# Routed layers: results scattered to their tokens' slots as they are made, and read back by plain loads

## What is computed

```python
x = x + jnp.tanh(g_xattn[i]) * _Li_xattn_ref(_layernorm(x), ctx, ...)
x = x + jnp.tanh(g_ffn[i])   * _Li_ffn_ref(_layernorm(x), ...)
```

```python
scores = jax.nn.softmax((xt @ gate_w.T).astype(jnp.float32), axis=-1)
_, idx = jax.lax.top_k(scores + gate_bias, TOPK)
weights = jnp.take_along_axis(scores, idx, axis=1)
y = jnp.zeros_like(xt)
for e in range(N_EXPERTS):
    gate_e = jnp.sum(jnp.where(idx == e, weights, 0.0), axis=1)
    h = jax.nn.silu(xt @ w1[e].T) * (xt @ w3[e].T)
    y = y + gate_e[:, None] * (h @ w2[e].T)
z = jax.nn.silu(xt @ sw1.T) * (xt @ sw3.T) @ sw2.T
return (y + z).reshape(shape)
```

## Time and profile before

| | before |
|---|---|
| median of three runs | 1986.92 us |
| lowest, highest | 1980.81, 1989.0 us |
| span of the profiled execution | 2007.2 us |
| busy: TensorE, VectorE, ScalarE, GpSimd | 1773.6, 1262.0, 975.4, 528.7 us |
| moved by SyncE's queue, by GpSimd's | 146.00, 30.69 MB |

### The profile page before, as it was taken

How to read it: one execution, slowest core, us unless ns; L and a number is a source line. 1 busy time by engine, 2 the same in 40 slices (tenths; PEclk the granted TensorE clock), 3 DMA queues, 4 the chain that set the end, 5 groups by cost and what they waited for, 6 DMA issues and landing times. The chain is left out here.

```text
span 2007.2 us, 32563 instructions
## 1 busy us (share of the span) xinstructions
PE 1773.6 (88%) x11808; PEld 1447.6 (72%) x11808; DVE 1262.0 (63%) x2310; ACT 975.4 (49%) x1739; POOL 528.7 (26%) x492
## 2 busy tenths in 40 slices
PE   6998899967799996699999969998899789798895
PEld 4667799922577775699999558886577566688884
DVE  6886488546245553588887566765434688656643
ACT  4652476413687671377776234443433255317730
POOL 2220343254333341222220630002000144213333
PEclk9998799988799996699999979999699899899997
DMA  3003377420100000567775220000000100026742
GB/s 109 17 17 126 121 255 248 132 61 0 49 1 12 6 12 25 203 225 229 246 238 169 81 102 1 1 1 1 22 1 1 57 12 12 30 79 208 235 127 81
DMA packets 97139, 178.32 MB, mean 89 GB/s; under 512 B 25184, under 2 KB 61946, under 8 KB 95914
## 3 DMA queue, kind: packets, MB, share of 16 engines
q1 hardware_dynamic: 85496, 146.00, 22.0%
q0 software_dynamic: 11232, 30.69, 5.2%
q10 hardware_dynamic: 288, 0.00, 0.0%
HBM read 149.38 MB, written 27.26 MB: 88 GB/s over the span
## 5 line engine op out<-in xcount | busy, mean ns | idle before, releaser
L1667 POOL DMA_INDIRECT f_block_rows_home<-normed_x,f_token_of_sb x138 | 168.3, 1220 | 451.4 <-PE psum L1713 324.5
L1693 PE MATMUL psum<-f_block_h_sb,f_w1h_home 128*128 128x256 f32 x736 | 211.4, 287 | 30.2 <-issue 10.7
L1693 PE MATMUL psum<-f_block_l_sb,f_w1h_home 128*128 128x256 f32 x736 | 206.8, 281 | 0.0
L1693 PE MATMUL psum<-f_block_h_sb,f_w1l_home 128*128 128x256 f32 x736 | 206.7, 281 | 0.0
L2316 PE MATMUL psum<-a_xT_home,context_w 128*128 128x256 f32 x704 | 182.2, 405 | 13.6 <-PEq L122 9.7
L1703 PE MATMUL psum<-f_w2h_home,f_hidden_h_home 128*128 128x256 f32 x644 | 187.4, 291 | 2.0 <-DVE f_hidden_l_home L1887 1.0
L1703 PE MATMUL psum<-f_w2h_home,f_hidden_l_home 128*128 128x256 f32 x644 | 181.7, 282 | 0.0
L1703 PE MATMUL psum<-f_w2l_home,f_hidden_h_home 128*128 128x256 f32 x644 | 181.7, 282 | 0.0
L1693 PEld LDWEIGHTS psum<-f_block_h_sb,f_w1h_home 128*128 128x128 f32 x736 | 140.8, 191 | 38.5 <-issue 28.6
L2316 PEld LDWEIGHTS psum<-a_xT_home,context_w 128*128 128x128 f32 x704 | 132.6, 198 | 45.3 <-issue 20.0
L2481 ACT ACTIVATE a_probsT_sb<-psum 77x1024 f32<-77x1024 f32 (+1 forms) x128 | 130.7, 1021 | 69.0 <-PE psum L2368 66.5
(11 more groups left out here) (314 smaller groups left out, 3986.6 us busy)
## 6 DMA issues: line engine op xcount, KB each, us to landing
f_w_sb<-in_f_w SPq DMA_DIRECT2D x161, 512.0 KB
sorted_y<-f_result_sb SPq DMA_DIRECT2D x69, 256.0 KB
normed_x<-f_xn_all SPq DMA_DIRECT2D x24, 256.0 KB, 2.1
f_b_row_sb<-in_f_b SPq DMA_DIRECT2D x46, 128.0 KB
f_w_sb<-in_f_w SPq DMA_DIRECT2D x23, 256.0 KB
f_block_rows_home<-normed_x,f_token_of_sb POOLq DMA_INDIRECT x138
residual<-in_x SPq DMA_DIRECT2D x8, 256.0 KB, 6.2
context_w<-in_a_wk SPq DMA_DIRECT2D x2, 1024.0 KB, 5.0
```

The lines of the kernel that those rows point to most:

```text
L1667: nc.gpsimd.indirect_dma_start(block_rows[b % 2][:, h, :], None, xs, bass.IndirectOffsetOnAxis(ap=column, axis=0)).then_inc(sems[f"rows_in ...
L1693: last = nc.tensor.matmul(hid_ps(q)[:, m, :], w, rhs, start=(j == 0), stop=(j == len(parts) - 1))
```

## The change

- A second table `slot_of` gives each row of each block a slot: that of its token's first or second choice, or a place of its own for a pad (from a table `pads` made once). It costs one operation of VectorE ahead of `token_of` and two behind it; the table `rows` and its cast go.
- `sorted_y` becomes `slots`, 4096 slots in the tokens' order with room for pads behind them. SyncE no longer stores results. GpSimd scatters each block, two scatters of 128 rows, when `result_out` says that it is made; it first issues the gathers of four blocks, then for each block b the gathers of block b+4 and the scatters of block b.
- `take_result` waits for both scatters of the block before last instead of the one store; six initial stores that raised its semaphore go, and four bodies of the loop are written out ahead of it in place of DEPTH.
- After the last scatter SyncE reads the slots back by plain loads of 256 KB, one for two tiles and one choice, 16 in a layer. In f0 there is room for 8 at first, and `slots_left` issues the other 8 as combinations free it. `combine` waits for these.
- In f0 and f1, SyncE waits for result b before it loads w2 of the last unit of block b+DEPTH. (Before, the same wait stood ahead of the store, behind both weights.)
- GpSimd's powers in f1 come one after another, with no gathers between them, and the null key and value of the next attention are loaded ahead of `slots_left`.

```diff
@@ find_rows
-        nc.vector.tensor_copy(t["rows"][:], rows_f[:].rearrange("p k t -> p (k t)")).then_inc(sems["rows_done"], 1)
...
+        step.did(nc.vector.tensor_scalar(unfilled[:], source[:], 0.0, None, ALU.is_equal))
         step.then(nc.vector.tensor_scalar(source[:], source[:], -1.0, 0.0, ALU.add, ALU.max))
         step.then(nc.vector.tensor_scalar(wrapped[:], source[:], float(TOKENS), -float(TOKENS), ALU.is_ge, ALU.mult))
         nc.vector.tensor_tensor(t["token_of"][:], source[:], wrapped[:], ALU.add).then_inc(sems["table_done"], 1)
+        step.then(nc.vector.tensor_tensor(unfilled[:], unfilled[:], env["pads"][:], ALU.mult))
+        nc.vector.tensor_tensor(t["slot_of"][:], source[:], unfilled[:], ALU.add).then_inc(sems["slots_done"], 1)
@@ routed_experts
+    LEAD = 4
...
-    RING = 8 if own else 16
...
+    RING = min(len(pairs), 2 * NBATCH)
@@ take_result
-        engine.wait_ge(sems[f"stored{s % 2}"], uses(i, s) * 16 + STORED0)
+        if not (isinstance(b, int) and b < 2):
+            engine.wait_ge(sems[f"stored{s % 2}"], uses(i, s) * (16 * BT))
@@ sync, weights
                 sp.dma_start(w1[k][:], dram[f"{name}_w1"][unit]).then_inc(sems[f"w_in{k}"], 16)
+                if freed and not silu and u == per_expert - 1:
+                    sp.wait_ge(sems["result_out"], (b - DEPTH) + (R0 + 1 + RESULT0))
                 sp.dma_start(w2[k][:], dram[f"{name}_w2"][unit]).then_inc(sems[f"w_in{k}"], 16)
@@ sync, body
-            sp.wait_ge(sems["result_out"], b + (R0 + 1 + RESULT0))
-            sp.dma_start(ys[bass.ds(b * BLOCK, BLOCK), :].rearrange("(h p) d -> p h d", p=P),
-                         result[s % 2][:]).then_inc(sems[f"stored{s % 2}"], 16)
             if what:
                 biases(what, s)
 
         run(sp, body)
+        for s in range(2):
+            sp.wait_ge(sems[f"stored{s}"], 16 * BT * len(range(s, BLOCKS, 2)))
+        for j in range(RING):
+            load_slots(sp, j)
+
+    def load_slots(sp, j):
+
+        b, k = divmod(j, 2)
+        first = k * TOKENS + b * SEQ
+        sp.dma_start(pairs[j % RING], slots[first:first + SEQ, :].rearrange("(h p) d -> p h d", p=P)).then_inc(
+            sems[f"slot_in{j % RING}"], 16)
+
+    def slots_left(sp):
+
+        for j in range(RING, 2 * NBATCH):
+            b, k = divmod(j - RING, 2)
+            sp.wait_ge(sems["combined"], (b * TPB + TPB - 1) * 2 + k + 1)
+            load_slots(sp, j)
@@ gpsimd
-        for s in range(2):
-            pool.wait_ge(sems[f"stored{s}"], STORED0 + 16 * len(range(s, BLOCKS, 2)))
+        def scatter(b):
+            pool.wait_ge(sems["result_out"], b + (R0 + 1 + RESULT0))
+            for h in range(BT):
+                column = t["slot_of"][:, b * BT + h:b * BT + h + 1]
+                nc.gpsimd.indirect_dma_start(slots, bass.IndirectOffsetOnAxis(ap=column, axis=0),
+                                             result[b % 2][:, h, :], None).then_inc(sems[f"stored{b % 2}"], 16)
+
+        for b in range(4):
+            gather(b)
+        pool.wait_ge(t["slots_done"], 1)
+        for b in range(BLOCKS):
+            if b + 4 < BLOCKS:
+                gather(b + 4)
+            scatter(b)
         rows = t["ahead"]["rows"] if t["ahead"] and t["ahead"]["between"] else None
-        for j in range(2 * TILES):
-            if j >= RING:
-                pool.wait_ge(sems["combined"], j - RING + 1)
-            if rows and j >= 8 and j % 4 == 0:
-                rows["power"](pool, j // 4 - 2, batch_tiles(j // 4 - 2))
-            col = (j % 2) * TILES + j // 2
-            nc.gpsimd.indirect_dma_start(gathered[j % RING], None, ys,
-                                         bass.IndirectOffsetOnAxis(ap=t["rows"][:, col:col + 1], axis=0)).then_inc(
-                                             sems[f"gathered{j % RING}"], 16)
-        for b in range(NBATCH - 2 if rows else NBATCH, NBATCH):
+        for b in range(NBATCH if rows else 0):
             rows["power"](pool, b, batch_tiles(b))
@@ combine
-            dve.wait_ge(sems[f"gathered{j % RING}"], 16 * (j // RING + 1))
+            pair = tile // TPB * 2 + k
+            dve.wait_ge(sems[f"slot_in{pair % RING}"], 16 * (pair // RING + 1))
```

More of the change, by code:

```diff
@@ L143, in build @@
         counting, marks = resident("counting", [P, P + 1]), resident("marks", [P, MARKS])
-        codes = resident("codes", [P, 2 * TILES])
+        codes, pads = resident("codes", [P, 2 * TILES]), resident("pads", [P, 2 * BLOCKS])
         context_w = resident("context_w", [P, 4 * DC * D * 2])
@@ L443, in load, with load_null @@
             sp.dma_start(dst, src).then_inc(sems["loaded"], 16)
+    def load_null(sp):
+        for dst, src in null:
+            sp.dma_start(dst, src).then_inc(sems["null_in"], 16)
     def load_late(sp):
         rows["load_late"](sp)
-        for dst, src in null:
-            sp.dma_start(dst, src).then_inc(sems["null_in"], 16)
         if hd == 64:
@@ L758, in vector @@
                 values_out(dve, j)
-    return dict(own=own, load_early=load_early, load=load, load_late=load_late, normalise_start=normalise_start,
+    return dict(own=own, load_early=load_early, load=load, load_null=load_null, load_late=load_late, normalise_start=normalise_start,
                 normalise_power=normalise_power, normalise_apply=normalise_apply, turn=turn, turned_out=turned_out,
@@ L973, in _ @@
                 t["operands_left"](sp)
+                ahead["load_null"](sp)
+                t["slots_left"](sp)
                 ahead["load_late"](sp)
             else:
+                t["slots_left"](sp)
                 t["store_output"](sp)
@@ L1474, in routed_experts @@
     nc, dram, psum, x, ident = env["nc"], env["dram"], env["psum"], env["x"], env["ident"]
-    xs, ys = env["normed_x"], env["sorted_y"]
+    xs, slots = env["normed_x"], env["slots"]
     name, per_expert = cfg["name"], cfg["per_expert"]
@@ L1517, in routed_experts @@
     result = [sb(f"result{s}", [P, BT, D]) for s in range(2)]
-    gathered = [w1[j // 4][:].rearrange("p c i -> p (c i)")[:, j % 4 * D:(j % 4 + 1) * D] for j in range(RING)]
+    whole = result + block_T + [v[:, k:k + BT, :] for v in w2[0:0 if own else len(w2)] for k in range(0, HC, BT)]
+    pairs = [v[:].rearrange("p a d -> p (a d)").rearrange("p (h d) -> p h d", d=D) for v in whole]
+    pairs += [v[:, c, :].rearrange("p (h d) -> p h d", d=D) for v in w1[0:2 if own else len(w1)] for c in range(DC)]
+    RING = min(len(pairs), 2 * NBATCH)
     def rows_places(attention):
@@ L1541, in routed_experts @@
          "block_low", "rounded", "lowered", "rows_in1", "stored0", "stored1"]
-        + [f"{kind}_in{k}" for k in range(DEPTH * per_expert) for kind in "wb"] + [f"gathered{k}" for k in range(RING)])}
+        + [f"{kind}_in{k}" for k in range(DEPTH * per_expert) for kind in "wb"] + [f"slot_in{k}" for k in range(RING)])}
     OUT = 1 if silu else HB
-    MULTIPLIED0, HIDDEN0, RESULT0, STORED0, READY0 = 2, 2 * OUT, 1, 16, 2 * HB
+    MULTIPLIED0, HIDDEN0, RESULT0, READY0 = 2, 2 * OUT, 1, 2 * HB
     hid_ready = sems["hid_ready"]
@@ L1556, in run @@
         rounds = (BLOCKS - max(DEPTH, 3)) // DEPTH
-        for b in range(DEPTH):
-            body(b, 0, b, max(DEPTH, 3))
-        with engine.Fori(1, rounds) as i:
+        for b in range(LEAD):
+            body(b, b // DEPTH, b % DEPTH, max(DEPTH, 3))
+        with engine.Fori(LEAD // DEPTH, rounds) as i:
             for s in range(DEPTH):
@@ L1661, in gpsimd, with gather @@
         pool.wait_ge(t["table_done"], 1)
-        for b in range(BLOCKS):
+        def gather(b):
             if b >= 2:
@@ L1930, in combine @@
                 nc.vector.bn_stats(env["stats"][:, tile - 1, :], x[:, tile - 1, :]).then_inc(sems["stated"], 1)
-            nc.vector.scalar_tensor_tensor(x[:, tile, :], gathered[j % RING],
+            nc.vector.scalar_tensor_tensor(x[:, tile, :], pairs[pair % RING][:, tile % TPB, :],
                                            t["chosen_gates"][:, k, tile:tile + 1], x[:, tile, :],
@@ L2130, in _ @@
             step.then(nc.vector.tensor_scalar(position[:], counting[:, P:P + 1], 1.0, None, ALU.add))
+            step.then(nc.vector.tensor_scalar(env["pads"][:], marks[:, 0:2 * BLOCKS], float(2 * TOKENS - 1), position[:],
+                                              ALU.add, ALU.add))
             step.then(nc.vector.tensor_scalar(codes[:], counting[:, 0:2 * TILES], float(P), position[:], ALU.mult, ALU.add))
```

22 lines of the change are left out of this document (11 added, 11 removed).

## The result

| | before | after |
|---|---|---|
| median | 1982.61 us (20 runs) | 1990.05 us (20 runs) |
| ratio to before | | 1.0037, 95% interval 1.0022 to 1.0051 |
| span of the profiled execution | 2007.2 us | 1986.2 us |
| GpSimd busy | 528.7 us | 622.9 us |
| ScalarE's waits for weights in f0's loop | 0.9 us | 50.0 us |

The change makes the kernel slower by 0.37%, some 7 us; the forecast was 0.3% faster. The two spans mislead: the execution of before that was profiled has a span some 25 us above the median of the timed runs. A second profile of the same kernel has a span of 1980.5 us, and is used for the comparison from here on (its run stands first among the experiments).

What follows compares the result with a forecast made beforehand. TensorE was taken to fill or nearly fill the block loops, GpSimd's row gathers to pace f1's tail. −8.5 + 0 + 0 + 2 + 0.2 = −6.3 us from 1986.9 gave about 1981 us, range 1969 to 1996.

Steps and rivals of the forecast that it cites:

- Step 4: SyncE's wait for a result ahead of the w2 load: +2 us in f0, nothing in f1.
- L: Time the awaited 512 KB w2 load takes in f0 and f1: taken as 3.5 us, upper bound 4.58.
- The circle: One-block loop in f0, result to w2 load to casts to next result: 3.2 to 3.66 us + L against 6.80.
- rival C: The w2 load closes the one-block loop in f0 and f1: about 1998 us, 2010 at L = 4.58; chance 0.12.
- rival B: GpSimd becomes the bound of a block loop, scatters at 1.65 us: about 1990 to 1992 us; chance 0.13.
- Step 1: Gathers out of f1's tail, leaving TensorE's 5.5 us for two tiles as the pace: −8.5 us.
- the 11.5 us behind the last value: In f1's tail, from taking the last value to the next stage's start: forecast to stay as it was.
- Step 2: Tails of f0 and f3: 0 us each, as what the combinations gain is covered.
- The cover: In f0's tail, VectorE's 21.02 us idle for ScalarE, taken to hide what the combinations gain.
- Step 3: Stores off SyncE, scatters on GpSimd in the block loops: 0 us, upper bound 9 in f0 and some 2 in f3.
- Step 5: Small edits around the tables, initial stores and GpSimd's order: 0, but +0.2 us once for the pads table.
- rival D: Stalls like ScalarE's 7.50 us idle belong to the row gathers and go too: −6 to −20 us more; chance 0.15.

Runs made afterwards that it cites:

- the last three runs: Kernel before with half of f1's row gathers, ratio 0.9995; with f1's powers issued behind four gathers, 1.0005; with both, 0.9968.
- the wait moved: Kernel after, with SyncE's wait for result b moved from ahead of the w2 load to behind it: 1976.74 us, ratio 0.9962 to before.
- the third scatter: Kernel after with SyncE's wait behind the w2 load, plus one small extra scatter for each block of f0: 1996.38 us, ratio 1.0061.

## Why the prediction was wrong

*Step 4, the new wait, is the one that failed, by one term: L.* The circle and its place were right, and its fixed part nearly so (3.2 to 3.66 forecast, 2.94 measured from result end to result end without the load, as SyncE was quicker by 0.15 and the cast's slack was used). The period, 6.80 by rows 13, is 6.70 on the mean. L was put at 3.5 and is 4.54 on the mean in f0. With 3.5 the circle would be 6.44 us and cost nothing; from L = 3.76 on it costs, and each of the 19 loads then counts with its whole length. About 3.5 is what a load takes that little disturbs: 12 of 19 take 3.5 to 3.7 once the gathers are small. I had interpolated between rows 11, medians of loads in stages where little else moves, while rows 2 show the DMA engines 81% busy in this loop. The one row from a block loop, 4.58 in rows 14, was taken for an upper bound, and it was near f0's mean. But a busy loop alone doesn't give L. The window of f1's loop after, with the columns of rows 2:

```profile
855.00:1088.00 233.00, 231.36 (x1977) 230.60 (x1976) 191.67 (x198) 160.43 (x277) 117.09 (x76) 1.00 0.72 235
```

The DMA engines are 72% busy there, and the load issued behind a result took only 3.4 to 4.0 us to its cast, 3.6 on the mean of the first 20 blocks. f0 was forecast at +2 and is +11 to +14 (its bound, for L = 4.58, had been +18); f1 at 0 and is +2 to +3 (bound +14), since L there is the 3.6 forecast, and 8.0+3.6 is just under the period of 11.65 (what makes the 2 to 3 us was not traced further). That is rival C. I gave it 0.12 for 1998 to 2010; it came, at some two thirds to three quarters of its price in f0 and next to nothing in f1. (By the formula for 4.58, its price at L = 4.3 would have been +15 in f0 and not +11.) The time of 1990.05 is the one that rival B named, 1990 to 1992; that is chance, as the runs without the wait show.

*Step 1* was right in size: −8.5 forecast, −7.2 to −7.7 measured, and the values are taken at 2.75 us each as the products come. The work gained the 8.8 us; that the 11.5 us behind the last value stay was not so, they became 12.7. The reason was half of the truth, as the last three runs show. *Step 2* was right: f0's stretch from the last result to the next stage is 127.3 us after and 128.7 in the second profile of before, though the combinations there take 31 us and not 39. The cover was thinner than rows 7 say, since one of the stalls lay in it: VectorE's idle time before the reduction is 8.75 us in the second profile of before and 17.11 after, 8.4 more, which is what the combinations gained. f3's tail is 60.7 and 62.4 us in the two profiles of after, against 62.0.

*Step 3*: a scatter takes 1.38 us on the mean, within 0.95 to 1.65, though single ones take up to 2.06. GpSimd's load in f0 came out at 6.7 us a block with the wait moved, right at the period, and cost nothing, as taken. That so little was left over I had not seen; the third scatter shows it. In f3 the loop keeps its length (116.2 us after, 116.1 before). Rival B decided nothing here.

The Trainium skill's rule on descriptors behind VectorE's two-port operations ("SBUF — State Buffer", section "SBUF: two separate sides") is borne out further than the prediction says. Rows 12 and 13 can't speak against the cast: the gather at 312.01 began 0.20 us ahead of it. Where the cast is first, it does hold the issue up. VectorE and GpSimd in the trace of before:

```profile
238.43 0.69 DVE L1903 CAST f_hidden_h_home<-f_hidden_sb 128x1024 fp32r<-128x1024 f32 x1
238.50 1.43 POOL L1667 DMA_INDIRECT f_block_rows_home<-normed_x,f_token_of_sb  x1 [0.30 <-issue]
...
312.94 1.22 DVE L1887 TENSOR_TENSOR f_hidden_l_home<-f_hidden_sb,f_hidden_h_home 128x1024 fp32r<-128x1024 f32 x1
```

The cast had 0.62 us to go when the issue began, and 1.43 is 0.62+0.81. The subtraction of two SBUF inputs at 312.94 had 0.83 to go at 313.33, and the gather's 1.65 is 0.83+0.82. In the traces of before, after and the wait moved, 404 issues begin while such an operation has more than 0.15 us to go. 384 of them take what is left of it and 0.80 to 0.88 us, all 31 behind a cast among them; 19 issues behind a tensor operation with an input in PSUM took 0.95 to 0.99, whatever was left. By this the scatters do pay on GpSimd's queue (1.38 us on the mean, 0.97 undisturbed), but with the wait moved they cost f0's loop nothing.

*Step 5* and *rival D*: the small edits don't show. The stalls of rows 9 belonged to one execution. The base of the sum was the median of three runs, 1986.9; twenty runs gave 1982.6. Without the wait's +2 the sum was −8.3 us, a ratio of 0.9958; the kernel with the wait moved has 0.9962 (0.9948 to 0.9976). So the rest of the sum was right.

## What to carry to other kernels

When an edit moves a wait ahead of a load, look for a circle through the load, and then ask for the load's mean in that very loop, not for its time elsewhere: once the circle is the longest path, each block takes the fixed part and its own load. A semaphore shared by two loads makes the first user of the one wait for the other: giving w2 its own was worth as much as moving the wait. A wait's total says little of its price: 50 us of ScalarE's waits cost f0's loop 14 us, and 62 in f1's cost 3. Where an engine seems to pace a stretch at 6.3 us, read what ended its short idle times too; a circle of the same length can stand beside its work, and then taking away either wins little.

## What the runs showed of the hardware

A 512 KB load issued into f0's loop, with the DMA engines busy 76% of the time (239 GB/s), took 3.4 to 6.7 us from issue to use, 4.54 on the mean, with the long ones at nearly the same places in both profiles of the kernel; in f1's loop, at 72% and 235 GB/s, it took 3.4 to 4.0. With the row gathers' traffic cut from 256 to 16 KB a block, the ordinary ones in f0 fell to 3.5 to 3.7 and the long ones stayed. GpSimd's issue of a gather or scatter of 128 rows took 0.94 to 0.97 us alone, and up to 2.06 behind a cast or a subtraction of VectorE whose inputs all lie in SBUF. Two profiles of one kernel differed by 26.7 us in their spans (2007.2 and 1980.5) through stalls that no instruction explains, so a second profile of before is worth its run ahead of any account by stages.
